# Attention of layers 2 and 3 with folded weights, in two interleaved halves

## The reference

```
layer 2:  Q = xn Wq' + bq;  K = ctx Wk' + bk;  V = ctx Wv' + bv
          x += softmax(Q K' / sqrt(128)) V
layer 3:  qp = xn Wq' + bq; kp = ctx Wk';      vp = ctx Wv' + bv
          x += (softmax(qp kp' / sqrt(128)) vp) Wo' + bo
```

## Time and profile before

| | us |
|---|---|
| median of 3 runs | 982.84 (980.15 to 983.64) |
| profiled execution | 983.73, its span 981.7 |
| PE busy | 912.8 (93%) |
| DVE busy | 723.3 (74%) |
| POOL busy | 572.7 (58%) |
| ACT busy | 518.3 (53%) |

### The profile page before, as it was taken

One profiled execution on the slowest core, in us unless ns is written; L12 is line 12 of the kernel. 1 busy time (PEld: TensorE's weight loads), 2 busy tenths in 40 slices (PEclk: granted clock), 3 DMA queues, 4 the chain that ended last, 5 costly groups with the idle time before them and its releaser, 6 DMA issues. The chain is left out here.

```text
span 981.7 us, 16426 instructions
## 1 busy us (share of the span) xinstructions
PE 912.8 (93%) x4948; PEld 704.9 (72%) x4948; DVE 723.3 (74%) x1656; ACT 518.3 (53%) x986; POOL 572.7 (58%) x542
## 2 busy tenths in 40 slices
PE   7897998988898799999999999999999889999796
PEld 4556675666697756888888888888887766677564
DVE  6997776999456798766666666666667888886865
ACT  3455666544643256666666666666664334453354
POOL 5512544677513156777777777777776538884500
PEclk9999999999999889999999999999999689999998
DMA  6000000322000000000000000000002000000001
GB/s 193 1 2 2 1 1 11 87 71 67 12 1 27 1 9 14 25 25 24 24 24 24 24 24 24 24 24 24 25 4 108 1 1 1 1 1 1 1 11 33
DMA packets 27112, 24.01 MB, mean 24 GB/s; under 512 B 3419, under 2 KB 23987, under 8 KB 26803
## 3 DMA queue, kind: packets, MB, share of 16 engines
q1 hardware_dynamic: 27059, 23.34, 7.9%
HBM read 22.28 MB, written 1.05 MB: 24 GB/s over the span
## 5 line engine op out<-in xcount | busy, mean ns | idle before, releaser
L1766 PE MATMUL psum<-xw 128*128 128x512 f32 x1248 | 322.9, 395 | 3.9 <-DVE xw L1398 2.6
L665 POOL TENSOR_TENSOR hh<-arena,hh 128x512 fp32r<-128x512 f32 x176 | 228.0, 1296 | 82.1 <-ACT hh L813 80.4
L1766 PEld LDWEIGHTS psum<-xw 128*128 128x128 f32 x1248 | 232.5, 188 | 55.9 <-issue 7.2
L1602 DVE TENSOR_TENSOR psum<-psum,arena 128x512 f32<-128x512 f32 x176 | 123.1, 699 | 99.6 <-PE psum L1766 93.3
L1044 ACT ACTIVATE arena<-psum 128x512 f32<-128x512 f32 x176 | 105.4, 599 | 119.5 <-PE psum L1766 119.4
L813 ACT ACTIVATE hh<-arena 128x512 fp32r<-128x512 f32 x228 | 142.2, 625 | 47.8 <-DVE arena L1701 45.3
L1766 PE MATMUL psum<-hh,wdn 128*128 128x512 f32 x528 | 148.5, 390 | 0.2 <-POOL hh L665 0.2
L1607 DVE TENSOR_TENSOR arena<-psum,arena 128x512 f32<-128x512 f32 x176 | 121.7, 692 | 8.9 <-DVE psum L1602 2.9
L1766 PEld LDWEIGHTS psum<-hh,wdn 128*128 128x128 f32 x528 | 98.9, 188 | 21.0 <-POOL hh L665 0.5
L1766 PE MATMUL psum<-arena 128*32 128x128 f32 (+7 forms) x1032 | 96.5, 314 | 12.6 <-ACT arena L813 6.5
L1766 PEld LDWEIGHTS psum<-arena 128*32 128x32 f32 (+4 forms) x1032 | 71.6, 152 | 25.3 <-issue 11.7
(11 more groups left out here) (285 smaller groups left out, 1558.7 us busy)
## 6 DMA issues: line engine op xcount, KB each, us to landing
egu<-in_w SPq DMA_DIRECT2D x44, 128.0 KB, 2.0
egu<-in_egu SPq DMA_DIRECT2D x16, 256.0 KB, 2.6
edn<-in_w SPq DMA_DIRECT2D x44, 64.0 KB, 1.8
edn<-in_edn SPq DMA_DIRECT2D x16, 128.0 KB, 2.1
arena<-in_w SPq DMA_DIRECT2D x1, 1536.0 KB, 6.9
X<-in_x SPq DMA_DIRECT2D x4, 256.0 KB, 5.0
arena<-in_conv SPq DMA_DIRECT2D x1, 1024.0 KB, 8.9
out<-X SPq DMA_DIRECT2D x4, 256.0 KB, 2.3
```

The lines of the kernel that those rows point to most:

```text
L665: pool.tensor_tensor(hh[:, s % 4, 1, :], h1[:, s % 2, :], hh[:, s % 4, 0, :].bitcast(F32), ALU.subtract).then_inc(hh_lo, 1)
L1602: dve.tensor_tensor(bank(2 + k), bank(2 + k), sil[:, k, :], ALU.mult).then_inc(prod_done, 1)
L1766: return pe.matmul(dst, lhsT=lhsT, rhs=rhs, start=start, stop=stop)
```

## The change: what it does

- `Q K'` is computed as `xn (Wq' K')` plus a bias row: the keys of layer 2 and layer 3 (`k2T`, `k3T`) are multiplied by the untransposed query weights (`kq2`, `kq3`), and the query bias enters by a product of a broadcast tile (`bqB`) with the keys. `project` and its DVE copies are gone. In layer 3 `(P V) Wo'` becomes `P (V Wo')`: `v3T` times `wo3` gives `vo3`, and `c3T` is gone; `bo` is a bias row of it. The scale goes into the exponential.
- Keys, values and folded tiles of layer 3 are made in layer 2's attention and behind it.
- Context tiles are held twice in the partitions (`ctx_twice`), so that values exist in both halves of the partitions and one transpose takes the two tiles of a batch (8 instead of 16 transposes, on 128 rows).
- Scores, softmax, exponentials, transposes and outputs go in two halves of 8 tiles, the second interleaved with the outputs of the first. PE's fillers stay in front of the norm's transposes of L = 6 only.
- POOL normalises group 3 as well (L = 4 and 6), DVE only group 2.
- The high and low halves of layer 2's weights are made in four and two pieces; the second low piece waits for the routing weights. `w2all` and `ctx_twice` are loaded in layer 1, behind the first `hid_done`.
- One preload of the Sigmoid table goes (layer 1) and two stand in layer 2.

Its core (new functions whole, the rest cut):

```diff
 # SP, ahead of the loop that loads layer 1's chunks
+            sp.wait_ge(hid_done, 1)
+            sp.dma_start(w2all, A["w2"]).then_inc(w2_in, 16)
+            sp.wait_ge(ctx_in, 16)
+            sp.dma_start(ctx_twice.rearrange("p b j -> p (b j)"), A["ctxTd"]).then_inc(ctx_in, 16)
 # norms on POOL
-            return (L == 0 and g > 0) or (L in (1, 5) and g < NG - 1) or (L in (4, 6) and g < 2)
+            return (L == 0 and g > 0) or (L in (1, 5) and g < NG - 1) or (L in (4, 6) and g != 2)
 # POOL
+            def w2_low(part):
+                c = slice(NC2 // 2 * part, NC2 // 2 * (part + 1))
+                pool.wait_ge(wgu_hi, STEPS0 + NC1 + 1 + part)
+                pool.tensor_tensor(w2r[:, 1, c], w2all[:, c], w2r[:, 0, c].bitcast(F32), ALU.subtract).then_inc(wgu_lo, 1)
                 if L == 5:
-                    pool.wait_ge(x_done, NT * L)
+                    pool.wait_ge(rw_done, NG + 1)
+                    w2_low(1)
                     experts2_low()
 # ACT
-            load_table(ACT.Sigmoid)
+            def exponentials(n, hf):
+                act.wait_ge(sim_sub, 2 * n + hf + 3)
+                act.activation(e2[:, 8 * hf:8 * hf + 8, :], s2[:, 8 * hf:8 * hf + 8, :], ACT.Exp, scale=float(D) ** -0.5).then_inc(sim_exp, 1)
+                act.wait_ge(e2_tp, 2 * n + hf + 1)
+                copy(e2T[:, 512 * hf:512 * hf + 512], bank(PAIRS_T[n] + hf)).then_inc(e2_sb, 1)
...
+            ln_evac_group(4, 2)
+            w2_high(2)
+            exponentials(0, 0)
+            ln_evac_group(4, 3)
...
             load_table(ACT.Exp)
+            for g in range(NG - 1):
+                ln_evac_group(6, g)
+            exponentials(1, 0)
+            ln_evac_group(6, NG - 1)
+            exponentials(1, 1)
 # DVE
+            def attended(n, L):
+                softmax(n, 0)
+                denominators(n, 0)
+                for t in range(NT):
+                    if t == 4:
+                        softmax(n, 1)
+                    if t == 8:
+                        denominators(n, 1)
+                    dve.wait_ge(av2_ready, n * NT + t + 1)
+                    dve.scalar_tensor_tensor(X[:, t, :], psum[:, ATTENDED[n] + t % 4, 0:D], rden2[:, t:t + 1], X[:, t, :], ALU.mult, ALU.add)\
+                        .then_inc(x_done, 1)
+                    norm_behind(L, t)
 # PE
+            def values(hf, into, w, row):
+                mm(bank(into).rearrange("p (b d) -> p b d", d=D), ones[0:1, :],
+                   rows[0:1, ROW[row], :].unsqueeze(1).broadcast_to([1, B // 2, D]), True, False)
+                for b in range(B // 2 * hf, B // 2 * (hf + 1)):
...
+            mm(bank(4), wk2[:, :], ctxT[:, :]).then_inc(qk2_mm, 1)
+            busy(7, 3)
+            ln_transpose(4, 0)
+            pe.wait_ge(qk2_sb, 1)
+            mm(bank(5), wq2[:, :], k2T).then_inc(qk2_mm, 1)
+            query_bias(0, 0, k2T)
+            ln_transpose(4, 1)
+            pe.wait_ge(ctx_in, 32)
+            values(0, 6, wv2, "v2_b")
+            pe.wait_ge(qk2_sb, 2)
+            scores(0, 4, 0, kq2)
+            query_bias(0, 1, k2T)
+            ln_transpose(4, 2)
+            values(1, 7, wv2, "v2_b")
+            pe.wait_ge(v2_sb, 1)
+            pairs_T(0, 0)
+            ln_transpose(4, 3)
+            for t in range(4):
+                attend(0, 4, t, v2)
+            scores(0, 4, 1, kq2)
+            mm(bank(4), wk3[:, :], ctxT[:, :]).then_inc(qk2_mm, 1)
+            for t in range(4, 8):
+                attend(0, 4, t, v2)
+            pe.wait_ge(v2_sb, 2)
+            pairs_T(0, 1)
+            mm(bank(5), wv3[:, :], ctxT[:, :]).then_inc(qk2_mm, 1)
+            for t in range(8, NT):
+                attend(0, 4, t, v2)
+                if t == 11:
+                    pe.wait_ge(qk2_sb, 3)
+                    mm(bank(4), wq3[:, :], k3T).then_inc(qk2_mm, 1)
+            for hf in range(2):
+                pe.wait_ge(qk2_sb, 4 + hf)
+                values(hf, 5 - hf, None, "o3_b")
...
+            ln_transpose(6, 0)
+            ln_transpose(6, 1)
+            pe.wait_ge(ln_xnT, NG * 6 + 2)
+            query_bias(1, 0, k3T)
+            scores(1, 6, 0, kq3)
+            query_bias(1, 1, k3T)
+            ln_transpose(6, 2)
+            pe.wait_ge(ln_xnT, NG * 6 + 3)
+            pairs_T(1, 0)
+            ln_transpose(6, 3)
+            for t in range(4):
+                attend(1, 6, t, vo3)
+            scores(1, 6, 1, kq3)
+            for t in range(4, 8):
+                attend(1, 6, t, vo3)
+            pairs_T(1, 1)
+            for t in range(8, NT):
+                attend(1, 6, t, vo3)
```

More of the change, by code:

```diff
@@ new lines, in w2_high @@
+            def w2_high(part):
+                c = slice(NC2 // 4 * part, NC2 // 4 * (part + 1))
+                return copy(w2r[:, 0, c], w2all[:, c])
+            load_table(ACT.Exp)
+            for n, name in enumerate(("q2_b", "q3_b")):
+                act.activation(bqB[:, n, :], ones[:, :], ACT.Copy, scale=cols[:, COL[name]:COL[name] + 1])
+            act.wait_ge(qk2_mm, 1)
+            act.activation(k2T, bank(4), ACT.Identity, bias=cols[:, COL["k2_b"]:COL["k2_b"] + 1]).then_inc(qk2_sb, 1)
@@ new lines, in _ @@
+            w2_high(2)
+            exponentials(0, 0)
+            ln_evac_group(4, 3)
+            act.wait_ge(v2_mm, 2)
+            copy(v2[:, B // 2:B, :].rearrange("p b d -> p (b d)"), bank(7)).then_inc(v2_sb, 1)
+            w2_high(3).then_inc(wgu_hi, 1)
+            act.wait_ge(qk2_mm, 3)
+            copy(k3T, bank(4)).then_inc(qk2_sb, 1)
+            exponentials(0, 1)
+            load_table(ACT.Sigmoid)
+            act.wait_ge(qk2_mm, 4)
+            act.activation(v3T.rearrange("p b (r j) -> p b r j", r=2), twice(bank(5)), ACT.Identity,
+                           bias=cols[:, COL["v3_b"]:COL["v3_b"] + 1]).then_inc(qk2_sb, 1)
@@ L1618, in _ @@
             output_groups(4, 0)
[L1621 to L1641, removed]
-                    dve.tensor_tensor(s2[:, r, :], sim, wide(mx2[:, r].unsqueeze(2), 8, C), ALU.subtract).then_inc(sim_sub, 1)
-                for hf in range(2):
-                    r = slice(8 * hf, 8 * hf + 8)
-                    dve.wait_ge(sim_exp, base + hf + 3)
-                    then(dve.tensor_reduce(den2[:, r], e2[:, r, :], AX.X, ALU.add))
-                    then(dve.reciprocal(rden2[:, r], den2[:, r]))
@@ L1650, in _, with softmax @@
[L1650 to L1657 removed]
+            def softmax(n, hf):
+                r = slice(8 * hf, 8 * hf + 8)
+                sim = bank(SCORES[n] + hf).rearrange("p (t j) -> p t j", j=C)
+                dve.wait_ge(sim_mm, 2 * n + hf + 3)
+                then(dve.tensor_reduce(mx2[:, r], sim, AX.X, ALU.max))
+                dve.tensor_tensor(s2[:, r, :], sim, wide(mx2[:, r].unsqueeze(2), 8, C), ALU.subtract).then_inc(sim_sub, 1)
@@ new lines, in pairs_T, with attend @@
+            def pairs_T(n, hf):
+                pe.wait_ge(sim_exp, 2 * n + hf + 3)
+                for b in range(4 * hf, 4 * hf + 4):
+                    last = pe.transpose(psum[:, PAIRS_T[n] + hf, P * (b % 4):P * (b % 4) + P],
+                                        e2[:, TB * b:TB * b + TB, :].rearrange("p r j -> p (r j)"), ident[:, :])
+                last.then_inc(e2_tp, 1)
+            def attend(n, L, t, vals):
+                b, own = t // TB, slice(C * (t % TB), C * (t % TB) + C)
+                pe.wait_ge(e2_sb, 2 * n + t // 8 + 1)
+                if n == 0 and t == 3:
+                    pe.wait_ge(ln_xnT, NG * L + NG)
+                if t >= 4:
+                    pe.wait_ge(x_done, L * NT + t - 3)
+                mm(psum[:, ATTENDED[n] + t % 4, 0:D], e2T[own, P * b:P * b + P], vals[own, b, :]).then_inc(av2_ready, 1)
```

176 lines of the change are left out of this document (65 added, 111 removed).

## The result

The changed kernel takes 969.51 us (967.67 to 972.40, 4 runs) against 982.09 (980.15 to 983.64, 4 runs) of the kernel before on the same chip: ratio 0.9876, interval 0.9844 to 0.9907. The forecast was 971.0.

A forecast was written before the change was run, and what follows sets the result against it. PE was busy 93%, but the latency of a serial attention chain was taken to bound layers 2 and 3. Terms 3.1 - 8.4 + 2.2 - 9.8 + 0.5 = -12.4 took 983.73 to 971.3, forecast 971, range 964.5 to 979.

The forecast's parts named there:

- Layer 1's load: Layer 1: chunk 2's weights queue behind the early w2 and context loads and land near 390.5, so ACT waits: +3.1 us.
- PE has two units ahead and none to catch up with: Layer 1 step: PE cannot absorb ACT's wait for chunk 2, so the whole delay counts, +3.1 us.
- Layer 2: Layer 2's attention to the router's sigmoid: the reordered chain brings the sigmoid to 775.4 against 783.81, -8.4 us.
- I take the upper level: Layer 2: PE's clock assumed to stay at 2.4 GHz; at the lower level the last stretch costs 5.5 us more.
- rival 1: PE's clock falls again before layer 2's router: +5.5 us, 976.5 us in total; chance 0.20.
- Port contention: Before layer 2's combine copies: POOL's second w2 low piece holds DVE's products of two SBUF tiles, +2.2 us.
- Layer 3: Layer 3's attention: first addition -11.5 us, first convolution at 907.8 against 917.59, -9.8 us.
- +0.5 for slow convolutions: Layer 3: dropped fillers leave PE with nothing at 898 to 901, so the convolutions start slowly, +0.5 us (0 to 2).
- Rival 3: Layers 2 and 3: interleaving fails, each half waits for the other, half of 18.2 us lost: 980 us; chance 0.09.
- Rival 2: One or both new costs, layer 1's load wait and DVE held by POOL, do not arise: about 966 us; chance 0.16.
- Rival 4: Slower: PE at half clock bounds layer 2, low stretch over 12 us of PE-bound work: 990 us; chance 0.05.

The follow-up runs named there:

- kernel 1: The kernel before with only the w2 load moved early, behind layer 1's first hid_done, without the doubled context: 981.91 us, ratio 1.0008.
- kernel 2: The changed kernel with the loads of chunks 2 and 3 issued ahead of w2 and the doubled context: 966.54 us, ratio 0.9854.
- kernel 6: The changed kernel with 12 more fillers ahead of the first and second transposes of layer 2's attention: 972.66 us, ratio 0.9913.
- kernel 9: The changed kernel measured and profiled a second time, unedited: 968.28 us, ratio 0.9862.
- kernel 10: The changed kernel with the edits of kernel 2 and kernel 3 together: 964.28 us, ratio 0.9822.
- kernel 11: Kernel 10 with 4 fillers for 3 ahead of layer 2's first transposes and 3 more ahead of the second: 963.99 us, ratio 0.9823.
- kernel 3: The changed kernel with the second low half of w2 on POOL released by the last norm instead of the routing weights: 967.20 us, ratio 0.9869.
- kernel 7: The changed kernel with 34 more fillers in layer 3's attention: 969.93 us, ratio 0.9881.
- kernel 4: The changed kernel with layer 3's attention in one piece, not interleaved, folded weights kept: 980.92 us, ratio 0.9975.
- kernel 12: Kernel 4 with short fillers fitted into TensorE's waits in layer 3: 975.12 us, ratio 0.9925.

## Why the prediction was right, and where it was off

The time was right, and the four larger terms arose where they were laid out. Two of them were mis-sized: the load and the clock in layer 2.

- **Layer 1's load** (+3.1 forecast, +1.8 measured, 1.3 in the second profile). Order of the queue and landing time were right. The term is 0.2 above its own step, since 390.9 is 2.9 behind 387.98. The failed step is "PE has two units ahead and none to catch up with": there are 2.2 us of slack, shown by kernels 1, 2, 6 and 9.
- **Layer 2** (-8.4 forecast, -5.45 measured). The step that failed is "I take the upper level". The low level came twice, and not where rival 1 had it alone: at 777, with most of the router's last 16 products still to do, and at 749.5, ahead of the first additions. Where the clock holds, stretch 2 is 12.15 (-8.0) and stretch 3 is 19.33 (-0.3). Put together from different executions these make -8.3, so the steps laid out by hand came out to 0.1 in the sum and the mis-sized term is the clock, 2.8 us in the first profile. No profiled execution had both. In all eight profiles of the changed kernel and its variants without the reordered loads or fillers in layer 2 the clock fell there, about 2 us behind a wait of 0.83 us. The four transposes stand right behind that wait; the products of 64 columns come only behind the fall. The Trainium skill (TensorE: Matmul & The Clock Gate, Part 4) says that transposes don't count as busy for the clock in the way other products do. Transposes stand ahead of both falls, which agrees with it, but they stand as well in kernels 2, 10 and 11, where the clock held, and no run separates them from the wait.
- **Port contention** (+2.2 forecast, +1.9 measured). Right, shown by kernel 3, down to the step: the second product was held, and ended 0.55 behind POOL.
- **Layer 3** (-9.8 to the first convolution forecast, -11.0 measured; first addition -11.5 and -11.4). Right. The 1.2 lie behind the first addition, and +0.5 for slow convolutions was +0.2 (to the end of the program, which differs by as much between executions). The low level costs nothing there, as kernel 7 shows. Rival 3 put 9.1 us of both layers on the interleaving. In layer 3 alone it is worth 4.9, and 10.7 where the clock falls without it (kernels 4 and 12), and it did work.
- **Rival 2** (966 without the two new costs) did not come in the changed kernel; kernel 10 takes both costs out and has 964.3. **Rival 1**'s condition did come, a fall ahead of the sigmoid, and both falls together cost about half of its 5.5. Rival 4 did not come: the low stretches in layer 2 were 3.4 and 6.8 us long.
- That the sum came within 1.5 us is luck in part, for errors of both signs met: 1.3 + 1.2 + 0.3 + 0.3 too pessimistic, 2.95 too optimistic, and 0.8 of the profiles' difference lies where the code is all but the same.

What stays open: why the clock held at 748 in all three kernels whose layer 1 lost nothing (2, 10, 11) and fell in the eight profiles of the others. TensorE's rows from 741 on are the same. Layer 2's gain was not taken apart as layer 3's was: how much of it is the folding and how much the halves, no run shows. Nor is it known which executions of kernel 6 lost the clock, and where.

## What to carry to other kernels

Lay a reordered latency chain out by hand, at the upper level of the clock and at the lower, and keep the difference as a term of its own: it was the largest error here, while the chain at the upper level came out right to 0.1 us in the sum. A large early load belongs behind the next small ones in an in-order queue, and a GpSimd tensor operation away from VectorE's products of two SBUF operands; both edits are one or a few lines and came with 4.0 us together, 3.2 of it in their own stretches. A chain that leaves TensorE waiting pays twice, once for the wait and once for the clock behind it.

## What the runs showed of the hardware

- The rows right ahead don't decide the granted clock: behind the same rows and waits it was 1.00 in kernel 10 and 0.50 in kernel 9. Executions of one kernel differ too: kernel 4's ten had a mean granted clock of 0.957 to 0.967 and took 982.4 to 973.2 us, and the changed kernel's two profiles differ by 1.7 us in stretch 2.
- In layer 3's whole order (kernel 4) the clock fell at 884.6, behind waits of 0.8 and 1.4 us, and stayed at 0.50 although TensorE was busy without a gap from 885 to 896 with bias products of 512 columns and scores of 64. With the waits filled (kernel 12) the stretch was 5.9 us shorter.
- Three products of two SBUF operands took 5.13 us beside a GpSimd operation of 3.82 and 1.89 without it; GpSimd itself took 3.82 instead of 3.45. The product that started after GpSimd's operation was the one held, to 0.55 us behind that operation's end.
- A load of 128 KB issued behind 2 MB on the same queue let its reader start 7.8 us after issue; issued ahead of them (kernel 2) it made nobody wait.
